# Block transposes on VectorE in place of TensorE transposes in the last phase of a Fourier-operator kernel

## The chip, the cores and the metric

One NeuronCore of a Trainium2 chip runs the whole kernel as one program. The metric is the device time of one execution in microseconds; the times shown are medians of runs. TensorE is called PE (its weight loads PEld), VectorE DVE, ScalarE ACT, GpSimd POOL, and SyncE SP. Accumulators lie in PSUM, here as four tensors of two banks each (pA, pT, pD, pS); everything else lies in SBUF.

## What is computed

An image of 64 x 64 pixels and 3 channels goes through a spectral network (64 images, width 32, four layers), and the result, read as 4096 tokens of 64 numbers, goes through four token layers (attention, experts, a recurrent layer, experts). The change touches the end of the first part and the image load:

```
h = layer_norm(x @ fc0_w + fc0_b)
for i in range(4):
    h = spectral_conv(h, w1[i], w2[i]) + conv1x1(h, conv_w[i]) + conv_b[i]
    h = layer_norm(h)
    if i < 3: h = gelu(h)
h = gelu(h @ fc1_w + fc1_b)     # 32 -> 128
h = gelu(h @ fc2_w + fc2_b)     # 128 -> 64
h = (h @ fc3_w + fc3_b)[..., 0] # 64 -> 1
```

All values are float32.

## The kernel before, in words

**Groups and bodies.** The 64 images are worked on in 16 groups of 4. A group in the last spectral layer consists of steps with short names: `i1.0` and `i1.1` (inverse transform in y), `acc.0` to `acc.3` (inverse transform in x and the 1x1 convolution, accumulated in pA), a copy of each `acc` to SBUF by ACT (the tile `raw`), `sq` (squares, ACT), `red` (sums, DVE), `rs` (reciprocal root, seven small DVE operations, L207 to L213), `scale` (normalising `raw`, DVE, L1638), `turn.0` to `turn.3`, then the output layers `fc1.0` to `fc1.7`, `fc2.0` to `fc2.15`, `fc3.0`, `fc3.1`, `fin.0` and `fin.1`.

**What turn and fin do.** `raw[n]` holds rows (pixels) on partitions. `turn.n` (PE, L1317) makes eight 128 x 128 transposes of it into pA, and DVE copies pA to the tile `h_new` (L1646). `fin.h` (PE, L1405) makes four 128 x 128 transposes of `G3`, the copied result of `fc3.h`, into a half of pT, and two ACT instructions add the bias and put the wanted columns into the token tile (L1513).

**The output layers.** `fc1.u` (L1374) reads 512 columns of `h_new` in four strips of 32 partitions: strips 0 and 1 write the two banks of pD, strips 2 and 3 the two banks of pS. ACT takes pD and pS in one GELU each (L1496, `fc1.2u` and `fc1.2u+1`) into two buffers `G1`. `fc2.m` (L1385) reads one of these and writes a half of pT; ACT's GELU (L1499) takes it to one of eight slots of `G2`. `fc3.h` (L1395) reads eight slots, ACT copies the result to `G3` (L1502).

**Order.** Each engine has its own instruction queue, and the order of the steps in each queue is written out by hand in the table `ORDER`, for each phase. A trailing minus marks a step of the group before. The order `into_last` ends the layer before and starts group 0 of the last phase. Then a body runs the output layers of one group beside the image work of the next: 15 bodies in the order `last` (one by itself, fourteen in a loop), and after them a body with the late steps of the last group alone. Before the first body come the mixing matmuls of the layer (L1217) and POOL's store of their result, after which POOL clears the tiles of the token parameters. PE's order in a body, before:

```
fc2.0- fc1.1- fc2.1- i1.1 fc2.2- fc1.2- fc2.3- turn.2- fc2.4- fc1.3- fc2.5- i1.0 fc2.6- fc1.4-
fc2.7- turn.3- fc3.0- fc1.5- fc2.8- fc2.9- acc.0 fc2.10- fc1.6- fc2.11- acc.1 fc2.12- fc1.7- acc.2
fc2.13- fc2.14- acc.3 fc2.15- fin.0- turn.0 fc3.1- fc1.0 fin.1- turn.1
```

**Waits.** PSUM tensors are handed out as rings: pA (ring "a", one slot) to `i1`, `acc` and `turn`, the halves of pT (ring "r", two slots) to `fc2`, `fc3` and `fin`. A PE step waits until the one that had its slot before is taken. `fc1.u` waits for the copy of `turn.(u//2)` and until both GELUs of the `fc1` before have read pD and pS; `fc2.m` waits for the GELU of `fc1` into its buffer; `fc3.h` waits until ACT has taken its eight `fc2`; `acc.n` waits for DVE's transpose of `i1` (L1617).

Of the kernel before, what the change touches and what calls it, by code (L numbers as in the profile page):

```python
# [51 lines left out]
def constants():  # L52
# [77 lines left out]
    "h_new":         (4, 0, 4, 4),  # L130
    "x_in":          (16, 0, 0, 0),
    "y_in":          (0, 0, 128, 128),
# [25 lines left out]
    "into_last": {  # L158
        "PE": ("i1.1 turn.2- back.1- i1.0 acc.0 turn.3- back.2- acc.1 back.3- acc.2 f1.1- f1.0- acc.3 f2.0- f2.1- "
               "mix.0 turn.0 fc1.0 turn.1"),  # L160
        "ACT": ("gelu.2- back.1- acc.0 sq.0 gelu.3- back.2- acc.1 sq.1 back.3- acc.2 sq.2 acc.3 sq.3 pack.0- pack.1- "
                "mix.0 fc1.0 fc1.1"),
        "DVE": ("red.3- i1.1 rs.3- scale.3- i1.0 red.0 rs.0 scale.0 red.1 rs.1 f1.1- scale.1 red.2 f1.0- f2.0- f2.1- "
                "mix.0 turn.0"),
    },
    "last": {
# [9 lines left out]
    },  # L176
# [4 lines left out]
    "mid": dict(i1="d", back="s", f1="d", f2="d"),  # L181
    "last": dict(i1="a", acc="a", turn="a", fc2="r", fc3="r", fin="r"),
}
# [32 lines left out]
def build(nc, ins, out_ap, B):  # L216
# [18 lines left out]
    with ctx:  # L235
# [77 lines left out]
        def param(rows, cols):  # L313
# [47 lines left out]
                 "w_centred", "mix_a_full", "mix_a_free", "mix_b_full", "mix_b_free", "y_bias", "conv_cleared", "conv_loaded", "conv_turned", "conv_chain", "cst_loaded", "ln_loaded",  # L361
                 "fc0_loaded", "fc0_chain", "mlp_cleared", "mlp_loaded", "normed", "eps_set"]
        names += ["td_full", "td_free", "ts_full", "ts_free", "par_cleared", "par_loaded", "tok_ready", "v_chain", "shifted",
# [171 lines left out]
        def token_act(act):  # L535
# [8 lines left out]

            act.wait_ge(s["r_free"], 20 * NG + 2)
            act.sem_inc(s["tok_ready"], 1)
# [423 lines left out]
        def _(sp):  # L970
            def load_x(g):
                src = ins["x"].rearrange("(g t b) y x c -> g (b y) t (x c)", t=2, b=2)
                sp.dma_start(x_in, src[g]).then_inc(s["x_loaded"], 16)

# [35 lines left out]
            def mlp_params():  # L1010
                sp.wait_ge(s["mlp_cleared"], 1)
                for j in range(4):
                    sp.dma_start(fc1_w[32 * j:32 * j + 32, :],
                                 ins["L0_tok_fc1_w"]).then_inc(s["mlp_loaded"], 16)
                sp.dma_start(fc1_b, ins["L0_tok_fc1_b"].rearrange("(p o) -> p o", o=1)).then_inc(s["mlp_loaded"], 16)
                sp.dma_start(fc2_w, ins["L0_tok_fc2_w"]).then_inc(s["mlp_loaded"], 16)
                for j in range(2):
                    q = slice(64 * j, 64 * j + 64)
                    sp.dma_start(fc2_b[q], ins["L0_tok_fc2_b"].rearrange("(p o) -> p o", o=1)).then_inc(s["mlp_loaded"], 16)
                    for k in range(2):  # L1020
                        sp.dma_start(fc3_pad[q, k, 2 * k + j:2 * k + j + 1], ins["L0_tok_fc3_w"]).then_inc(s["mlp_loaded"], 16)
                sp.dma_start(fc3_b, ins["L0_tok_fc3_b"].partition_broadcast(P)).then_inc(s["mlp_loaded"], 16)
# [161 lines left out]
        def _(pe):  # L1184
# [43 lines left out]
            def steps(p):  # L1228
# [12 lines left out]
                def xt(n, g):  # L1241

                    pe.wait_ge(s["x_loaded"], at("x_in", ph, L, g, 16))
                    bank = bank_of("xt", n, g)
# [62 lines left out]
                def turn(n, g):  # L1307

                    pe.wait_ge(s["normed"], at("normed", ph, L, g, n + 1))
                    if ph == "last":  # L1310
                        bank = bank_of("turn", n, g)
                    else:
                        bank = pT
                        if n >= 1 or not first_group(g):
                            pe.wait_ge(s["h_new_ok"], at("h_new", ph, L, g, n))
                    for j in range(8):
                        mm = pe.transpose(bank[:, 128 * j:128 * j + 128], raw[n][:, 128 * j:128 * j + 128], ident)  # L1317
                    if ph == "last":
                        send(mm, "turn", n, g)
                    else:  # L1320
                        mm.then_inc(s["turned"], 1)

# [39 lines left out]
                def fc1(u, g):  # L1362
# [25 lines left out]
                def fc3(h, g):  # L1388
# [10 lines left out]
                def fin(h, g):

                    p.taken(pe, ("fc3", h), g=g)
                    alone(pe)
                    bank = bank_of("fin", h, g)
                    for j in range(4):
                        mm = pe.transpose(bank[:, 128 * j:128 * j + 128], G3[:, 128 * j:128 * j + 128], ident)  # L1405
                    send(mm, "fin", h, g)
# [9 lines left out]
        def _(act):  # L1416
# [18 lines left out]
            def steps(p):  # L1435
# [64 lines left out]

                def fc3(h, g):
                    act.copy(G3, take("fc3", h, g)).then_inc(s["r_free"], 1)  # L1502

                def fin(h, g):

                    bank = take("fin", h, g)
                    if first_group(g):
                        act.wait_ge(s["y_stored"], 64 * 2 * LAYERS)
                    alone(act)
                    out = tok[:, bass.ds(g * 128, 128)].rearrange("p (t a q n) -> p t a q n", t=2, a=4, q=4)  # L1510
                    src = bank.rearrange("p (q a t r) -> p t a q r", q=4, a=2, t=2)
                    for t in range(2):
                        ins_ = act.activation(out[:, t, 2 * h:2 * h + 2], src[:, t, :, :, 0:4], ACT.Identity, bias=fc3_b)  # L1513
                    ins_.then_inc(s["r_free"], 1)

# [7 lines left out]
        def _(dve):  # L1523
# [84 lines left out]
            def steps(p):  # L1608
# [85 lines left out]
```

## Time and profile before

| what | value |
| --- | --- |
| median of three runs | 3279.34 us (3277.0 to 3285.81) |
| span of the profiled execution | 3279.2 us |
| PE busy | 2937.9 us (90%) |
| PE weight loads busy | 1867.7 us (57%) |
| DVE busy | 2145.9 us (65%) |
| ACT busy | 1950.3 us (59%) |
| POOL busy | 61.9 us (2%) |

The profiled execution's own time is its span, 3279.2 us from the first to the last instruction; outside it no separate number is shown. Busy times overlap between engines. "Idle before" names the time that an engine stood still ahead of an instruction and what ended it. A timeline row gives the start, the length, the instruction with its output and input tiles, and how many neighbours are merged into it; PE records of neighbouring instructions overlap, so a pitch is best taken from starts. The last phase runs from about 1905 to 2659 us.

### The profile page before, as it was taken

Reading aid. Unit: us, or ns where it says so; the run is one execution under the profiler, and the core shown is the slowest. Engines: PE = TensorE matmul, PEld = TensorE weight load, DVE = VectorE, ACT = ScalarE, POOL = GpSimd, SP = SyncE. Lnnn points to the kernel's source line nnn. Section 1 sums busy time; section 2 is a strip of 40 time slices with the busy share of each in tenths; the row PEclk is TensorE's granted clock in tenths of the full one; section 3 lists DMA queues with packets and bytes.
Section 4 is the critical chain, followed back from the end, with each engine's and each line's share of the span. In section 5 each row is a group of like instructions: output and inputs, shape, how many; then the busy total and the mean of one; then the engine's idle time right before and its main releaser. Section 6 shows DMA issues by size and latency. Waiting matters only on the chain.

```text
span 3279.2 us, 82177 instructions
## 1 busy us (share of the span) xinstructions
PE 2937.9 (90%) x32240; PEld 1867.7 (57%) x32240; DVE 2145.9 (65%) x3954; ACT 1950.3 (59%) x2271; POOL 61.9 (2%) x81
## 2 busy tenths in 40 slices
PE   7888889999889999889999889999999987964994
PEld 3545466666666666666666544444444447952893
DVE  6888668888668888668888644454445434255457
ACT  6777656666556666556666457777777753422451
POOL 0000000000000000000000010000000001000000
PEclk9999999999999999999999999999999998986897
DMA  3422346544447544546544423111111000000000
GB/s 96 130 97 99 100 152 209 193 165 164 152 130 218 183 164 163 155 154 209 179 165 164 151 67 86 46 55 58 46 46 55 29 1 1 1 1 0 1 1 13
DMA packets 98093, 335.91 MB, mean 102 GB/s; under 512 B 29928, under 2 KB 61960, under 8 KB 62088
## 3 DMA queue, kind: packets, MB, share of 16 engines
q1 hardware_dynamic: 75400, 161.50, 16.4%
q10 hardware_dynamic: 18432, 134.23, 10.0%
q0 software_dynamic: 4096, 37.75, 5.3%
q8 instruction: 131, 2.15, 0.3%
q14 instruction: 34, 0.28, 0.0%
HBM read 179.29 MB, written 154.14 MB: 102 GB/s over the span
## 4 chain that ended last, share of the span: by engine, by line
PE 79%; DVE 11%; issue 5%; ACT 5%; DVEq 0%; SPq 0%; DMA 0%; ACTq 0%
PE pA L1291 15%; PE pA L1299 8%; PE pT L1385 8%; PE pT L1317 5%; PE pS L1328 5%; PE pD L1342 4%; PE pD L1374 4%; PE pD L1356 4%; PE pD L467 3%; PE pA L467 3%; PE pD L1263 3%; PE pA L1281 3%; PE pS L459 2%; PE pT L459 2%; DVE arena L1657 2%
## 5 line engine op out<-in xcount | busy, mean ns | idle before, releaser
L1624 DVE TENSOR_REDUCE small<-arena 128x32 f32<-128x1056 f32 x320 | 397.0, 1241 | 316.0 <-ACT arena L1461 311.3
L1291 PEld LDWEIGHTS pA<-conv_bd,h_in 128*128 128x128 f32 x4096 | 479.0, 192 | 109.4 <-issue 92.7
L1291 PE MATMUL pA<-conv_bd,h_in 128*128 128x128 f32 x4096 | 517.4, 280 | 8.6 <-DVE arena L1617 2.9
L1451 ACT COPY w_sb<-pA 128x1024 f32<-128x1024 f32 x256 | 259.8, 1015 | 393.0 <-PE pA L1299 343.3
L1638 DVE SCALAR_TENSOR_TENSOR w_sb<-w_sb,small 128x1024 f32<-128x1024 f32 x320 | 386.8, 1213 | 5.5
L1472 ACT ACTIVATE h_new<-pT,bet,gam 128x1024 f32<-128x1024 f32 x256 | 307.5, 1201 | 100.2 <-PE pT L1317 92.1
L1461 ACT ACTIVATE arena<-w_sb 128x1024 f32<-128x1024 f32 x320 | 339.3, 1060 | 13.4
L1317 PEld LDWEIGHTS pT<-cst,w_sb 128*128 128x128 f32 x2048 | 225.2, 143 | 144.5 <-issue 123.9
L1317 PE MATMUL pT<-cst,w_sb 128*128 128x128 f32 x2048 | 283.0, 282 | 23.2 <-DVE w_sb L1638 23.2
L1476 ACT COPY h_rows<-pS 128x1024 f32<-128x1024 f32 x256 | 257.1, 1004 | 64.9 <-PE pS L1328 64.6
L1328 PEld LDWEIGHTS pS<-cst,h_new 128*128 128x128 f32 x2048 | 228.5, 143 | 113.0 <-issue 71.6
L1328 PE MATMUL pS<-cst,h_new 128*128 128x128 f32 x2048 | 275.4, 278 | 9.4 <-ACT h_new L1472 9.4
L1299 PE MATMUL pA<-arena,cst 64*64 64x512 f32 x2048 | 278.8, 615 | 0.0
L1385 PE MATMUL pT<-w_sb,arena 128*64 128x512 f32 x1024 | 270.3, 616 | 2.7 <-ACT w_sb L1499 1.5
L1356 PE MATMUL pD<-arena,cst 64*32 64x384 f32 (+1 forms) x4096 | 206.8, 491 | 10.2 <-DVE arena L1657 9.8
L1499 ACT ACTIVATE w_sb<-pT,arena 128x512 f32<-128x512 f32 x256 | 173.1, 685 | 16.5 <-PE pT L1385 15.4
L1496 ACT ACTIVATE w_sb<-pD,arena 128x1024 f32<-128x1024 f32 x128 | 142.5, 1113 | 63.1 <-PE pD L1374 39.3
L1657 DVE STREAM_TRANSPOSE arena<-pD 128x768 f32<-128x768 f32 x128 | 125.5, 981 | 78.4 <-PE pD L1356 62.5
L1342 PE MATMUL pD<-h_rows,cst 64*32 64x512 f32 x2048 | 139.7, 600 | 36.2 <-DVE arena L1651 21.2
L1651 DVE STREAM_TRANSPOSE arena<-pD 128x1024 f32<-128x1024 f32 x128 | 159.3, 1245 | 4.9 <-PE pD L1342 1.1
L1617 DVE STREAM_TRANSPOSE arena<-pD 128x1024 f32<-128x1024 f32 x96 | 119.8, 1248 | 47.9 <-PE pD L1263 47.3
L1374 PE MATMUL pD<-h_new,arena 32*128 32x512 f32 x512 | 145.5, 644 | 3.6 <-issue 1.7
(299 smaller groups left out, 3903.0 us busy)
## 6 DMA issues: line engine op xcount, KB each, us to landing
h_scratch<-h_new ACTq DMA_DIRECT2D x128, 1024.0 KB, 4.5
h_in<-h_scratch SPq DMA_DIRECT2D x128, 1024.0 KB, 5.1
y_scratch<-w_sb POOLq DMA_DIRECT2D x32, 576.0 KB, 8.4
y_in<-y_scratch SPq DMA_DIRECT2D x512, 36.0 KB
w_sb<-in_L_tok_w1r_dram POOLq DMA_DIRECT2D x8, 576.0 KB, 7.0
w_sb<-in_L_tok_w1i_dram POOLq DMA_DIRECT2D x8, 576.0 KB, 6.7
w_sb<-in_L_tok_w2r_dram POOLq DMA_DIRECT2D x8, 576.0 KB, 8.3
w_sb<-in_L_tok_w2i_dram POOLq DMA_DIRECT2D x8, 576.0 KB, 7.7
```

What stands on the lines that cost most here:

```text
L1291: pe.matmul(pA[:, c:c + 128], h_in[:, 1024 * n + c:1024 * n + c + 128], conv_bd[:], start=(j == 0), stop=False, skip_group_check=True)
L1299: mm = pe.matmul(pA[64 * b:64 * b + 64, 512 * t:512 * t + 512].rearrange("p (x o) -> p o x", o=C), const["idft_y"][rows, 64 * b:64 * b + 6 ...
L1317: mm = pe.transpose(bank[:, 128 * j:128 * j + 128], raw[n][:, 128 * j:128 * j + 128], ident)
L1328: mm = pe.transpose(bank[:, 128 * j:128 * j + 128], h_new[:, 1024 * n + 128 * j:1024 * n + 128 * j + 128], ident)
L1342: mm = pe.matmul(out[q:q + 32, b], const["dft_y"][rows, NQ * b:NQ * b + NQ], src[rows, t, 32 * xh:32 * xh + 32, 16 * ch:16 * ch + 16], sta ...
L1356: mm = pe.matmul(out.rearrange("p (q h c) -> p h c q", h=2, c=16), const["dft_x"][rows, 128 * part + 32 * j:128 * part + 32 * j + 32], TA[ ...
L1374: mm = pe.matmul(out, fc1_w[rows, :], h_new[rows, 512 * u:512 * u + 512], start=True, stop=True)
L1385: mm = pe.matmul(bank[64 * j:64 * j + 64, :], fc2_w, G1[m % 2][:, 512 * j:512 * j + 512], start=True, stop=True)
L1461: act.activation(sq[n % 2][:, :, 0:C], raw[n].rearrange("p (x o) -> p x o", o=C), ACT.Square, scale=float(C) ** -0.5).then_inc(s["squared" ...
L1472: act.activation(h_new[:, 1024 * n:1024 * n + 1024], pT[:], ACT.Gelu if ph == "mid" else ACT.Identity, bias=bet[:, col], scale=gam[:, col] ...
L1624: dve.reduce_sum(var[n], sq[n % 2], axis=AX).then_inc(s["summed"], 1)
L1638: dve.scalar_tensor_tensor(out=z, in0=z, scalar=ROOT_SCALE, in1=r.broadcast_to([P, 32, C]), op0=ALU.mult, op1=ALU.mult).then_inc(s["normed ...
```

## The change

In the last phase `turn` becomes one DVE block transpose (blocks of 32 x 32 on 128 partitions) from `raw` to `h_new`, and the PE transposes and DVE copies go. `fin` loses its PE part: DVE block-transposes `G3` into a new tile `G3_t`, and one ACT instruction takes the wanted columns. Because block transposes leave each strip of 32 partitions with other pixels than before, the image load is laid out anew (two DMAs of 64 partitions per group), `fc1`'s matmuls write their strips to other banks, and `fc3`'s take their slots of `G2` in another order. The rings lose `turn` and `fin`, the orders lose the PE steps, DVE gets `fc3.0-` and `fc3.1-`, and new waits stand in ACT's `acc`, `fc3` and `fin` and in DVE's `turn` and `fc3`.

```diff
-    "x_in":          (16, 0, 0, 0),
+    "x_in":          (32, 0, 0, 0),
...
     "into_last": {
-        "PE": ("... f2.1- mix.0 turn.0 fc1.0 turn.1"),
+        "PE": ("... f2.1- mix.0 fc1.0"),
...
     "last": {
-        "PE": the order quoted above
+        "PE": ("fc2.0- fc1.1- fc2.1- i1.1 fc2.2- fc1.2- fc2.3- fc2.4- fc1.3- fc2.5- i1.0 fc2.6- fc1.4- fc2.7- fc3.0- fc1.5- fc2.8- fc2.9- acc.0 fc2.10- fc1.6- fc2.11- acc.1 fc2.12- fc1.7- acc.2 fc2.13- fc2.14- acc.3 fc2.15- fc3.1- fc1.0"),
-        "DVE": ("rs.2- scale.2- turn.1- i1.1 red.3- turn.2- rs.3- scale.3- i1.0 turn.3- red.0 red.1 rs.0 rs.1 red.2 "
-                "scale.0 scale.1 turn.0"),
+        "DVE": ("rs.2- scale.2- turn.1- i1.1 red.3- turn.2- rs.3- scale.3- i1.0 turn.3- fc3.0- red.0 red.1 rs.0 rs.1 red.2 scale.0 turn.0 scale.1 fc3.1-"),
...
-    "last": dict(i1="a", acc="a", turn="a", fc2="r", fc3="r", fin="r"),
+    "last": dict(i1="a", acc="a", fc2="r", fc3="r"),
...
+        G3_t = w_sb[:, 3584:4096]
...
-                src = ins["x"].rearrange("(g t b) y x c -> g (b y) t (x c)", t=2, b=2)
-                sp.dma_start(x_in, src[g]).then_inc(s["x_loaded"], 16)
+                src = ins["x"].rearrange("(g b t) y x c -> g b y t (x c)", t=2, b=2)
+                for b in range(2):
+                    sp.dma_start(x_in[64 * b:64 * b + 64], src[g][b]).then_inc(s["x_loaded"], 16)
...
                 def fc1(u, g):
-                    for j in range(4):
-                        rows = slice(32 * j, 32 * j + 32)
-                        out = (pD, pS)[j // 2][:, 512 * (j % 2):512 * (j % 2) + 512]
...
+                    for k in range(2):
+                        for b in range(2):
+                            rows = slice(64 * b + 32 * k, 64 * b + 32 * k + 32)
+                            mm = pe.matmul((pD, pS)[k][:, 512 * b:512 * b + 512], fc1_w[rows, :], h_new[rows, 512 * u:512 * u + 512],
+                                           start=True, stop=True)
+                        mm.then_inc(s["s_full" if k else "d_full"], 1)
...
                 def acc(n, g):          # ACT
                     if ph == "last":
                         p.in_turn(act, "acc", n, g)
+                        if not first_group(g):
+                            act.wait_ge(s["h_new_ok"], at("h_new", ph, L, g, n - 3))
+                            alone(act)
...
                 def fc3(h, g):          # ACT
+                    if h or not first_group(g):
+                        act.wait_ge(s["g3_turned"], 2 * g + h)
+                        alone(act)
                     act.copy(G3, take("fc3", h, g)).then_inc(s["r_free"], 1)

                 def fin(h, g):          # ACT
-                    bank = take("fin", h, g)
+                    act.wait_ge(s["g3_turned"], 2 * g + h + 1)
...
+                    out = tok[:, bass.ds(g * 128, 128)].rearrange("p (b h n x) -> p b h n x", b=2, h=2, n=2)
+                    src = G3_t.rearrange("p (x r) -> p r x", r=32)[:, 0:4, :].rearrange("p (b n) x -> p b n x", b=2)
+                    act.activation(out[:, :, h], src, ACT.Identity, bias=fc3_b).then_inc(s["fin_done"], 1)
...
                 def turn(n, g):         # DVE
-                    p.in_turn(dve, "turn", n, g)
-                    dve.tensor_copy(h_new[:, 1024 * n:1024 * n + 1024], take("turn", n, g)).then_inc(s["a_free"], 1)
-                    p.taken(dve, ("turn", n), g=g)
-                    dve.sem_inc(s["h_new_ok"], 1)
+                    if not first_group(g):
+                        dve.wait_ge(s["s_full"], p.quad("s", 2 * n + 1, g - 1))
+                        alone(dve)
+                    dve.wait_ge(s["normed"], at("normed", ph, L, g, n + 1))
+                    dve.transpose(h_new[:, 1024 * n:1024 * n + 1024], raw[n]).then_inc(s["h_new_ok"], 1)
+
+                def fc3(h, g):
+
+                    p.taken(dve, ("fc3", h), g=g)
+                    if h or not first_group(g):
+                        alone(dve)
+                        dve.wait_ge(s["fin_done"], 2 * g + h)
+                    dve.transpose(G3_t, G3).then_inc(s["g3_turned"], 1)
```

## Rows read from the trace of the kernel before

**Rows 1.** Windows by engine: start:end, length, PE, PEld, DVE, ACT, POOL busy (count), clock, DMA.

```profile
1964.20:2623.60 659.40, 657.42 (x5043) 283.84 (x5042) 309.21 (x589) 510.03 (x645) 0.00 (x0) 1.00 0.18 52
...
2623.60:2659.40 35.80, 31.34 (x178) 9.21 (x178) 7.76 (x14) 28.04 (x39) 0.00 (x0) 1.00 0.00 1
```

**Rows 2.** Lines of the fourteen steady bodies: count, busy us, mean ns, idle before.

```profile
L1317 PE MATMUL pA<-cst,w_sb 128*128 128x128 f32 x449 | 59.9, 276 | 0.0
...
L1405 PE MATMUL pT<-cst,w_sb 128*128 128x128 f32 x112 | 18.4, 286 | 0.0
...
L1617 DVE STREAM_TRANSPOSE arena<-pA 128x1024 f32<-128x1024 f32 x28 | 34.9, 1246 | 37.5 <-PE pA L1263 37.5
```

**Rows 3.** Timeline of one steady body, PE, ACT and DVE: start, us, instruction.

```profile
2098.41 1.08 PE L1385 MATMUL pT<-w_sb,arena 128*64 128x512 f32 x4
...
2100.88 1.92 PE L1395 MATMUL pT<-w_sb,arena 128*32 128x512 f32 x16
...
2102.94 0.70 PE L1374 MATMUL pD<-h_new,arena 32*128 32x512 f32 x2
...
2102.95 0.70 PE L1374 MATMUL pS<-h_new,arena 32*128 32x512 f32 x2
...
2105.54 1.08 PE L1385 MATMUL pT<-w_sb,arena 128*64 128x512 f32 x4
...
2110.48 0.70 PE L1374 MATMUL pD<-h_new,arena 32*128 32x512 f32 x2
...
2113.59 1.08 PE L1385 MATMUL pT<-w_sb,arena 128*64 128x512 f32 x4
...
2119.59 1.08 PE L1385 MATMUL pT<-w_sb,arena 128*64 128x512 f32 x4
...
2121.69 1.92 PE L1395 MATMUL pT<-w_sb,arena 128*32 128x512 f32 x16
...
2102.87 0.59 ACT L1502 COPY w_sb<-pT 128x512 f32<-128x512 f32 x1 [1.34 <-PE pT L1395]
...
2103.11 0.18 DVE L207 TENSOR_SCALAR small<-small 128x32 int32<-128x32 int32 x1 [0.82 <-DVE h_new L1646]
...
2105.82 1.22 DVE L1646 COPY h_new<-pA 128x1024 f32<-128x1024 f32 x1
```

**Rows 4.** Timeline of PE in the late-only last body.

```profile
2624.59 0.70 PE L1374 MATMUL pD<-h_new,arena 32*128 32x512 f32 x2
...
2627.03 1.08 PE L1385 MATMUL pT<-w_sb,arena 128*64 128x512 f32 x4 [0.28 <-ACT w_sb L1496]
...
2628.11 0.70 PE L1374 MATMUL pD<-h_new,arena 32*128 32x512 f32 x2
...
2653.32 1.08 PE L1385 MATMUL pT<-w_sb,arena 128*64 128x512 f32 x4 [0.50 <-ACT w_sb L1499]
...
2655.28 1.92 PE L1395 MATMUL pT<-w_sb,arena 128*32 128x512 f32 x16 [0.29 <-ACT w_sb L1499]
```

**Rows 5.** Timeline of the entry into the last phase: PE, DVE, POOL.

```profile
1905.52 1.83 PE L1317 MATMUL pA<-cst,w_sb 128*128 128x128 f32 x8 [1.13 <-ACT w_sb L1432]
...
1907.50 1.23 DVE L1646 COPY h_new<-pA 128x1024 f32<-128x1024 f32 x1 [5.53 <-PE pA L1317]
...
1907.92 7.08 POOL L1173 MEMSET spec<- 128x8358 f32 x1
...
1909.03 1.22 PE L1374 MATMUL pD<-h_new,arena 32*128 32x512 f32 x2 [1.67 <-issue]
...
1909.08 5.97 DVE L207 TENSOR_SCALAR small<-small 128x32 int32<-128x32 int32 x1 [0.36 <-DVE h_new L1646]
...
1918.90 1.28 PE L1263 MATMUL pA<-y_in,cst 48*32 48x208 f32 x32 [3.00 <-issue]
...
1923.41 1.08 PE L1385 MATMUL pT<-w_sb,arena 128*64 128x512 f32 x4
```

**Rows 6.** Timeline of PE at the program's start.

```profile
14.07 3.75 PE L1281 MATMUL pA<-arena 128*128 128x512 f32 x4 [7.79 <-DVE arena L1539]
```

More of the change, by code:

```diff
@@ L158 @@
     "into_last": {
[L159 to L164, printed above, removed]
[3 rows of a table added]
     },
     "last": {
[9 rows of a table removed]
[3 rows of a table added]
     },
@@ L361, in build @@
                  "w_centred", "mix_a_full", "mix_a_free", "mix_b_full", "mix_b_free", "y_bias", "conv_cleared", "conv_loaded", "conv_turned", "conv_chain", "cst_loaded", "ln_loaded",
-                 "fc0_loaded", "fc0_chain", "mlp_cleared", "mlp_loaded", "normed", "eps_set"]
+                 "fc0_loaded", "fc0_chain", "mlp_cleared", "mlp_loaded", "g3_turned", "fin_done", "normed", "eps_set"]
         names += ["td_full", "td_free", "ts_full", "ts_free", "par_cleared", "par_loaded", "tok_ready", "v_chain", "shifted",
@@ L542, in take @@
                 return TS[(n[0] - 1) % 4]
-            act.wait_ge(s["r_free"], 20 * NG + 2)
+            act.wait_ge(s["fin_done"], 2 * NG)
             act.sem_inc(s["tok_ready"], 1)
@@ L1020, in mlp_params @@
                     for k in range(2):
-                        sp.dma_start(fc3_pad[q, k, 2 * k + j:2 * k + j + 1], ins["L0_tok_fc3_w"]).then_inc(s["mlp_loaded"], 16)
+                        sp.dma_start(fc3_pad[q, k, 2 * j + k:2 * j + k + 1], ins["L0_tok_fc3_w"]).then_inc(s["mlp_loaded"], 16)
                 sp.dma_start(fc3_b, ins["L0_tok_fc3_b"].partition_broadcast(P)).then_inc(s["mlp_loaded"], 16)
@@ L1241, in xt @@
                 def xt(n, g):
-                    pe.wait_ge(s["x_loaded"], at("x_in", ph, L, g, 16))
+                    pe.wait_ge(s["x_loaded"], at("x_in", ph, L, g, 32))
                     bank = bank_of("xt", n, g)
@@ L1309, in turn @@
                     pe.wait_ge(s["normed"], at("normed", ph, L, g, n + 1))
[L1310 to L1315, printed above, removed]
-                    for j in range(8):
[L1317 to L1321, printed above, removed]
+                    if n >= 1 or not first_group(g):
+                        pe.wait_ge(s["h_new_ok"], at("h_new", ph, L, g, n))
+                    for j in range(8):
+                        mm = pe.transpose(pT[:, 128 * j:128 * j + 128], raw[n][:, 128 * j:128 * j + 128], ident)
+                    mm.then_inc(s["turned"], 1)
                 def back(n, g):
@@ L1370, in fc1 @@
                     alone(pe)
-                    for j in range(4):
-                        rows = slice(32 * j, 32 * j + 32)
-                        out = (pD, pS)[j // 2][:, 512 * (j % 2):512 * (j % 2) + 512]
-                        mm = pe.matmul(out, fc1_w[rows, :], h_new[rows, 512 * u:512 * u + 512], start=True, stop=True)
-                        if j % 2:
-                            mm.then_inc(s["d_full" if j == 1 else "s_full"], 1)
+                    for k in range(2):
[4 more added lines that the diff above has]
+                        mm.then_inc(s["s_full" if k else "d_full"], 1)
                 def fc2(m, g):
@@ L1392, in fc3 @@
                     bank = bank_of("fc3", h, g)
-                    for k in range(2):
+                    for part in range(2):
                         for u in range(4):
-                            mm = pe.matmul(bank[32 * u:32 * u + 32, :], fc3_pad[:, k, :], G2[:, 2 * u + k, :],
-                                           start=(k == 0), stop=(k == 1), skip_group_check=True)
+                            mm = pe.matmul(bank[32 * u:32 * u + 32, :], fc3_pad[:, part, :], G2[:, 4 * part + u, :],
+                                           start=(part == 0), stop=(part == 1), skip_group_check=True)
                     send(mm, "fc3", h, g)
[L1399 to L1406, printed above, removed]
                 return dict(xt=xt, i1=i1, acc=acc, turn=turn, back=back, f1=f1, f2=f2,
-                            fc1=fc1, fc2=fc2, fc3=fc3, fin=fin)
+                            fc1=fc1, fc2=fc2, fc3=fc3)
             phases(pe, "PE", mix, steps)
@@ L1501, in fc3 @@
                 def fc3(h, g):
+                    if h or not first_group(g):
+                        act.wait_ge(s["g3_turned"], 2 * g + h)
+                        alone(act)
                     act.copy(G3, take("fc3", h, g)).then_inc(s["r_free"], 1)
                 def fin(h, g):
-                    bank = take("fin", h, g)
+                    act.wait_ge(s["g3_turned"], 2 * g + h + 1)
+                    alone(act)
                     if first_group(g):
                         act.wait_ge(s["y_stored"], 64 * 2 * LAYERS)
[L1509 to L1514, printed above, removed]
+                    out = tok[:, bass.ds(g * 128, 128)].rearrange("p (b h n x) -> p b h n x", b=2, h=2, n=2)
+                    src = G3_t.rearrange("p (x r) -> p r x", r=32)[:, 0:4, :].rearrange("p (b n) x -> p b n x", b=2)
+                    act.activation(out[:, :, h], src, ACT.Identity, bias=fc3_b).then_inc(s["fin_done"], 1)
                 return dict(xt=xt, acc=acc, sq=square, gelu=gelu, back=back, pack=pack, fc1=fc1, fc2=fc2, fc3=fc3, fin=fin)
@@ L1658, in f2 @@
                                   bank.rearrange("p (t n) -> p t n", t=2)[:, :, 0:384]).then_inc(s["d_free"], 1)
-                return dict(cen=cen, i1=i1, red=red, rs=rs, scale=scale, turn=turn, f1=f1, f2=f2)
+                return dict(cen=cen, i1=i1, red=red, rs=rs, scale=scale, turn=turn, fc3=fc3, f1=f1, f2=f2)
             phases(dve, "DVE", mix, steps, conv_centre, centring)
```

11 rows, old and new, of the table ORDER are left out of this document.

## Prediction

> **What bounds the kernel now.** I read the stretches first, then the waits inside them, then the order of one body. Fourteen steady bodies of the last phase fill 659.4 us, 47.1 us each; TensorE (PE) is busy for 657.42 us of that at clock 1.00, VectorE (DVE) for 309.21 and ScalarE (ACT) for 510.03 [rows 1]. So PE sets this phase, and PE work taken out can shorten it, but only as far as nothing else ends just behind it. "PE busy" does not show that; it is read from starts. The busy PE hides ACT: a GELU has to come back from ACT before PE may go on, and an instruction that stands in the gap looks like work, although the gap would be there without it. The late-only last body, which has no image work, shows it: PE idles 0.28 us in front of one fc2 and 0.29 us in front of fc3 [rows 4].
>
> **What is removed from PE, and what comes back.** Per body, 32 transposes of images and 8 of tokens go. Their busy time over 14 bodies is 59.9 and 18.4 us, so 4.28 and 1.31 us per body, 5.6 together [rows 2] (records of neighbours overlap, so the starts give some 0.5 less). If all of it came back, 15 bodies would give some 80 us. I take each place apart by starts in rows 3, against what the same chain needs where nothing stands between.
>
> - turn.2 between fc2.3 and fc2.4. fc2.4 needs the GELU of fc1.2's first bank. From the start of an fc1 to the fc2 that waits for its GELU the bare chain takes 2627.03 - 2624.59 = 2.44 us [rows 4]. From fc1.2 to fc2.4 it is now 2113.59 - 2110.48 = 3.11 [rows 3]. Gain 0.67, not the 1.0 of turn.2.
> - turn.3 between fc2.7 and fc3.0. fc3 waits for the GELU of the last fc2: bare, 2655.28 - 2653.32 = 1.96 [rows 4]; now 2121.69 - 2119.59 = 2.10 [rows 3]. Gain 0.14.
> - fin.0 and turn.0 between fc2.15 and fc3.1: now 2100.88 - 2098.41 = 2.47 [rows 3], bare 1.96. Gain 0.51.
> - fc3.1 to fc1.0 is 2.06; fc3's own pitch is at most its 1.92, with the overlap some 1.85 [rows 3]. fc1.0 waited for DVE's copy of turn.0, which now is early. Gain 0.14 to 0.21.
> - fin.1 and turn.1 between fc1.0 and fc2.0: now 2105.54 - 2102.94 = 2.60 [rows 3], bare 2.44. Gain 0.16, where 1.5 us of PE work go.
>
> Sum 1.62 to 1.69. Against it: an fc2 begun after a wait holds PE for 1.08 (2627.03 to 2628.11 [rows 4]), one that was queued for 1.01 or less; four places at 0.07 each make 0.28 at most. Per body 1.35 to 1.7, I take 1.5; fourteen bodies 21 us (19 to 24). What is late next at every place is ACT's GELU.
>
> **What DVE takes on.** Four copies from PSUM of 1.22 us [rows 3] become four block transposes from SBUF, and two transposes of 512 columns come in. No row has a 1024-column transpose from SBUF: bounds are a copy's 1.22 and double the 1.25 of the transpose from PSUM [rows 2], 2.5; I take 1.25, the same operation and size, and 0.7 for half. DVE has half of its time free [rows 1], so only one place counts. The transpose of G3 (fc3.1) waits for ACT's copy, and rs.2, scale.2 and turn.1 are queued behind it, and PE's fc1.2 behind turn.1. From fc3.1's start: ACT's copy at +1.99, 0.59 long, DVE at about +2.75, G3 done at +3.45, rs.2 and scale.2 take 2105.82 - 2103.11 = 2.71, turn.1 1.25: +7.4, with a semaphore +7.55 [rows 3]. PE reaches fc1.2 at 1.85 + 2.44 + (2110.48 - 2105.54) = +9.2. Slack 1.7 us, which the doubled price (1.95 more) would just use up: nothing, or 0.3 per body. ACT's fin waits for G3's transpose too, but two GELUs stand before it. ACT's copy of an image result gets a wait for the transpose of the group before, which ran a body earlier: nothing.
>
> **Banks of fc1 and fc3.** The same matmuls in another order. The four of fc1 begin 0.01 us apart in pD and pS [rows 3], together. Each keeps a row strip and a bank of its own, so I take nothing; the other bound is pairs one after the other, near 1 us for each of 128, and below zero there is no cause for a gain.
>
> **Entry into the phase.** After the mixing matmuls, PE runs turn.0 at 1905.52, once ACT has emptied its bank; DVE had been idle 5.53 us when it began the copy at 1907.50, so since 1901.97; fc1.0 begins at 1909.03 [rows 5]. Now DVE can transpose at 1902 and be done by 1903.4, and fc1.0 begins at 1905.5, when the bank is free: 3.5 us. Then rs.2's first operation took 5.97 us instead of 0.18, while a POOL memset from 1907.92 ran 7.08 us; that made turn.1 late, which holds pA, and PE sat 3.00 us in front of i1.1 at 1918.90 [rows 5]. With turn.0 done at 1903.4, rs.2 is through near 1905, turn.1 near 1907.5, before the memset, and i1.1 no longer waits for pA: 3.0 us. The PE records at 1909.03 are 1.22 long against 0.70 [rows 3, 5], so PE runs slowly there; the new first ops meet that too, and turn.1 as warm-up is gone. That may cost 1 to 2 us, the second slow spell behind the 3 us gap gives about as much back. Entry 6.5 us; between 3 (the stall stays) and 7.5.
>
> **The rest.** The first body's interior lacks some of the waits above: 1.1. The last body loses turn.2, 0.6; in its tail a PE turn is swapped for a DVE turn of like length. The image load becomes two DMA issues on SP; at the start PE's first accumulation waits for DVE's setup chain (7.79 us idle before 14.07 [rows 6]), behind which half a microsecond of SP is hidden, and later loads run a group ahead. If that cover were gone: one issue per group, well under 1 us each. Zero.
>
> **Sum:** 6.5 + 1.1 + 21 + 0.6 = 29.2 us from the profiled span of 3279.2, which lies 0.14 below the median of the runs, 3279.34. Forecast 3250.
>
> **PE's clock.** With 1.3 to 1.4 us waits at two places and 0.9 at two more, PE would be some 92% busy. In the last body PE is busy 31.34 of 35.8 us, 88%, with the same kind of gaps, and the granted clock is 1.00 [rows 1]. The Trainium skill ("TensorE: Matmul & The Clock Gate", "A second HAM failure mode: psum-queue depth-cycling") tells of a kernel whose short idles between matmul groups made the clock swing between its levels. By that rule the change would lose, the rival below; the rows speak against it.
>
> **Rivals.**
> 1. All of PE's removed time comes back: 3279 - 80 - 7 = 3192. For it: PE is the bound everywhere. Against it: the bare chains of rows 4. 3%.
> 2. The new queue on DVE: if the transposes from SBUF cost three times 1.25, turn.1 comes 3.9 us later, 2.2 past its slack, more than the body's 1.5. Entry gain only, some 3272 to 3282. Nothing but the missing row speaks for it. 6%.
> 3. Slower: PE's short waits bring the clock down. A PE instruction at the low level takes nearly twice as long. With a fifth of the 700 us at 1.2 GHz (mean 0.90) a tenth of the work is lost, some 76 us: 3250 + 76 = 3326. It decides from a mean clock of about 0.96, where it eats the 29 us. 5%. By the Trainium skill's rule on short idles this would be the outcome; rows 1 are against it.
> 4. The entry keeps its stall and bodies give 1.2: 3279 - 3 - 17 - 1 = 3258, inside the range.
>
> **Numbers.** The likeliest case with its variants holds 86%: 7.5 + 24 + 1.7 = 33 off gives 3246, 3258 the other end; the bounds of the transposes and the spread of runs (3277.0 to 3285.8) widen this to 3238 to 3264. A measurement here can tell about 0.3%, 10 us, from no change. Faster 0.86 (with rival 1), same 0.08, slower 0.06.
>
> **What would show it.** Right: bodies of about 45.6 us; PE idle before fc2.4, fc3.0, fc3.1 and fc2.0, each put down to an ACT GELU; no 3 us gap before i1.1; clock 1.00. Wrong: fc1.2 waiting for DVE; a granted clock under 0.97 in the steady bodies; an fc1 pitch over 1.1 us; bodies under 44 us.

## The result, and the profile after

| | before | after |
| --- | --- | --- |
| median | 3281.58 us (3277.0 to 3285.81) | 3260.07 us (3258.54 to 3262.73) |
| profiled span | 3279.2 us | 3256.7 us |

The ratio of the times is 0.9931, with a 95% interval of 0.9918 to 0.9944. The changed kernel is faster, by 21.5 us between the medians and 22.5 us between the profiled spans, where 29 were forecast. The measured 3260 lies inside the range and 10 us above the forecast figure; 2.2 of these 10 come from the median of the kernel before, which is 3281.58 here and was 3279.34 in the forecast. The medians and ratios below leave out four executions with a lower mean granted clock (3379.61 to 3673.02 us, one of the kernel before and one each in runs 5, 6 and 8), and of run 8 only the last phase is read, which lies ahead of the fall of its clock.

Cut at the same instructions, the two profiled executions give:

| stretch | before | after | gain | forecast |
| --- | --- | --- | --- | --- |
| start to last mixing matmul | 1903.28 | 1906.14 | -2.86 | 0 |
| last mixing matmul to fc2.3 | 20.13 | 13.85 | 6.28 | 6.5 |
| fc2.3 to the first steady body | 40.79 | 39.76 | 1.03 | 1.1 |
| fourteen steady bodies | 659.40 | 643.44 | 15.96 | 21 |
| last body, fc2.0 to fc3.1 | 31.68 | 31.01 | 0.67 | 0.6 |
| fc3.1 to the end | 623.92 | 622.50 | 1.42 | 0 |
| sum | 3279.2 | 3256.7 | 22.5 | 29.2 |

The windows of the kernel after, over its fourteen steady bodies and its last body (start:end, length, then busy time and count of PE, PEld, DVE, ACT, POOL, the granted clock, DMA), answer to [rows 1]:

```profile
1959.75:2603.19 643.44, 589.22 (x4481) 223.58 (x4481) 325.85 (x616) 508.84 (x617) 0.00 (x0) 1.00 0.18 54
2603.19:2638.31 35.12, 28.25 (x153) 6.76 (x154) 10.39 (x19) 27.74 (x36) 0.00 (x0) 1.00 0.00 1
```

PE is now busy 589.22 of 643.44 us, 91.6%, and the clock stays at 1.00. Some 68 us of PE's busy time went, 16 us of the time. The rest is PE's idle time, which the grouped lines of the same stretch put down to ACT's two GELUs (count | busy, mean ns | idle before and its releaser):

```profile
L1371 PE MATMUL pT<-w_sb,arena 128*64 128x512 f32 x897 | 236.1, 614 | 27.2 <-ACT w_sb L1476 27.2
...
L1381 PE MATMUL pT<-w_sb,arena 128*32 128x512 f32 x448 | 53.9, 598 | 28.4 <-ACT w_sb L1479 28.4
...
L1630 DVE STREAM_TRANSPOSE h_new<-w_sb 128x1024 f32<-128x1024 f32 x56 | 68.8, 1229 | 0.5
...
L1638 DVE STREAM_TRANSPOSE w_sb<-w_sb 128x512 f32<-128x512 f32 x28 | 19.9, 712 | 85.6 <-ACT w_sb L1485 85.6
```

The first two rows hold 55.6 us of idle, which accounts for all that PE has (643.44 - 589.22 = 54.2 by the windows). fc2 waits for the GELU of fc1 (L1476), fc3 for the GELU of fc2 (L1479). The last two rows give the prices that no row of before had: 1.23 us for a transpose of 1024 columns from SBUF, 0.71 for one of 512.

Timeline of one steady body of the kernel after, PE: fc2.0, fc1.2 and the fc2.4 that waits for it, fc2.7 and fc3.0, fc2.15 and fc3.1, fc1.0, the next fc2.0 and the fc1.1 behind it; it answers to [rows 3].

```profile
2097.69 1.08 PE L1371 MATMUL pT<-w_sb,arena 128*64 128x512 f32 x4 [1.43 <-ACT w_sb L1476]
...
2102.63 0.70 PE L1360 MATMUL pD<-h_new,arena 32*128 32x512 f32 x2
...
2105.20 1.08 PE L1371 MATMUL pT<-w_sb,arena 128*64 128x512 f32 x4 [0.42 <-ACT w_sb L1476]
...
2111.21 1.08 PE L1371 MATMUL pT<-w_sb,arena 128*64 128x512 f32 x4
2113.31 1.92 PE L1381 MATMUL pT<-w_sb,arena 128*32 128x512 f32 x16 [1.01 <-ACT w_sb L1479]
...
2137.14 1.08 PE L1371 MATMUL pT<-w_sb,arena 128*64 128x512 f32 x4
2139.24 1.92 PE L1381 MATMUL pT<-w_sb,arena 128*32 128x512 f32 x16 [1.01 <-ACT w_sb L1479]
2141.09 0.70 PE L1360 MATMUL pD<-h_new,arena 32*128 32x512 f32 x2
...
2143.66 1.08 PE L1371 MATMUL pT<-w_sb,arena 128*64 128x512 f32 x4 [1.43 <-ACT w_sb L1476]
2144.67 0.70 PE L1360 MATMUL pD<-h_new,arena 32*128 32x512 f32 x2
```

A body takes 2143.66 - 2097.69 = 45.97 us, in place of 47.1. PE stands at exactly the four places that were named. But the chains are longer than the bare ones that the sum used: fc1 to its waiting fc2 takes 2.57 twice (2105.20 - 2102.63, 2143.66 - 2141.09) where [rows 4] gave 2.44, and fc2 to fc3 takes 2.10 twice where they gave 1.96.

The entry into the phase in the kernel after answers to [rows 5]: turn.0 and rs.2's first operation on DVE, the last mixing matmul, fc1.0, POOL's first memset, fc2.0, i1.1, a second memset, fc1.2, a reduction on DVE, fc2.3, fc2.4, and a third memset with rs.3's first operation under it.

```profile
1905.02 1.23 DVE L1630 STREAM_TRANSPOSE h_new<-w_sb 128x1024 f32<-128x1024 f32 x1
...
1906.14 1.11 PE L1210 MATMUL pS<-w_sb,spec 64*32 64x64 f32 x53 [1.49 <-issue]
1906.18 0.14 DVE L198 TENSOR_SCALAR small<-small 128x32 int32<-128x32 int32 x1
...
1908.70 0.70 PE L1360 MATMUL pD<-h_new,arena 32*128 32x512 f32 x2 [1.45 <-ACT w_sb L1409]
...
1910.78 7.08 POOL L1166 MEMSET spec<- 128x8358 f32 x1
...
1911.12 1.97 PE L1371 MATMUL pT<-w_sb,arena 128*64 128x512 f32 x4 [1.28 <-ACT w_sb L1476]
...
1916.95 1.03 PE L1256 MATMUL pA<-y_in,cst 48*32 48x208 f32 x32
...
1917.92 3.51 POOL L1169 MEMSET h_rows<- 64x4096 f32 x1
...
1918.92 0.70 PE L1360 MATMUL pD<-h_new,arena 32*128 32x512 f32 x2
...
1919.36 1.21 DVE L1605 TENSOR_REDUCE small<-arena 128x32 f32<-128x1056 f32 x1
...
1919.99 1.08 PE L1371 MATMUL pT<-w_sb,arena 128*64 128x512 f32 x4
...
1921.35 1.08 PE L1371 MATMUL pT<-w_sb,arena 128*64 128x512 f32 x4 [0.28 <-ACT w_sb L1476]
...
1921.49 3.50 POOL L1171 MEMSET h_rows<- 1x4096 f32 x1
1921.64 3.39 DVE L198 TENSOR_SCALAR small<-small 128x32 int32<-128x32 int32 x1
```

turn.0 runs before the last mixing matmuls begin on PE and is through just behind their start, the first operation of rs.2 takes 0.14 us because it is through before the memset, and nothing idles before i1.1. The operation that a memset holds is now rs.3's (3.39 us), where nobody waits for it. PE has a slow spell of its own here: after two idles of 1.45 and 1.28 us the granted clock is 0.50, the lower of its two levels, from 1911.12 to 1915.00, and fc2.0 takes 1.97 us in place of 1.08. One more thing is to be seen here: this first body is not in the loop, and its chain from fc1.2 to fc2.4 is 1921.35 - 1918.92 = 2.43, as in [rows 4].

### The profile page after: what moved, and what is told of

Its sections match the earlier page's. It is cut to its first block, busy times and chain, and to the rows that moved or that the text cites. A ratio compares the mean times of both kernels' runs of the same rounds, so it can differ in the third digit from the quotient of the medians.

```text
span 3256.7 us, 80827 instructions
## 1 busy us (share of the span) xinstructions
PE 2861.2 (88%) x31600; PEld 1798.1 (55%) x31600; DVE 2161.4 (66%) x3986; ACT 1948.1 (60%) x2239; POOL 61.9 (2%) x81
## 4 chain that ended last, share of the span: by engine, by line
PE 76%; DVE 11%; ACT 7%; issue 5%; DVEq 0%; SPq 0%; DMA 0%; ACTq 0%
PE pA L1284 15%; PE pA L1292 8%; PE pT L1371 7%; PE pT L1306 5%; PE pS L1314 5%; PE pD L1328 4%; PE pD L1360 4%; PE pD L1342 4%; PE pD L459 3%; PE pA L459 3%; PE pA L1274 3%; PE pD L1256 3%; PE pS L451 2%; PE pT L451 2%; DVE arena L1647 2%
## 5 line engine op out<-in xcount | busy, mean ns | idle before, releaser
L1479 ACT ACTIVATE w_sb<-pT,arena 128x512 f32<-128x512 f32 x256 | 171.3, 685 | 8.0 <-PE pT L1371 6.3
L1476 ACT ACTIVATE w_sb<-pD,arena 128x1024 f32<-128x1024 f32 x128 | 142.4, 1112 | 55.4 <-PE pD L1360 31.6
L1371 PEld LDWEIGHTS pT<-w_sb,arena 128*64 128x64 f32 x1024 | 54.0, 135 | 213.8 <-issue 112.6
```

What stands on the lines that cost most here:

```text
L1371: mm = pe.matmul(bank[64 * j:64 * j + 64, :], fc2_w, G1[m % 2][:, 512 * j:512 * j + 512], start=True, stop=True)
```

## The experiments

**Theory before the runs:** PE's removed work comes back only where it exceeded ACT's round trip, and inside the loop each such stall costs about 0.13 us more than in the bodies that are written out. **Rivals:** the 0.13 belongs to the body (more neighbours, other work on ACT) and not to the loop; or the new transposes on DVE hold something.

**1. The changed kernel with its loop written out.**

```diff
-            with eng.Fori(2, NG) as b:
+            for b in range(2, NG):
                 at_body(b)
```

> The changed kernel with the fourteen steady bodies of the last phase written out instead of looped, so that every wait there is against a constant; nothing else. In the loop each place where PE waits for ACT takes 0.13 to 0.15 us more than the same place in the first and last bodies, which are not looped (2.57 against 2.43 us from an fc1 to the fc2 behind its GELU, 2.10 against 1.95 from an fc2 to fc3). Theory A, the loop's waits (values that PE's sequencer works out at the wait) make that difference: bodies fall from 45.97 to 45.4 us, the time by 7 to 8 us, to about 3252. Rival B, the difference is ACT's, from the image work beside it: bodies stay at 45.97, the time at 3260. Rival C, longer code has to be fetched and costs more than it gives: bodies above 46, time above 3262.

Measured: 3252.84 us (3252.14 to 3258.17), ratio to before 0.9915 (0.9898 to 0.9931). The timeline of PE in one body, from fc3.1 to the next fc3.1:

```profile
2089.64 1.92 PE L1381 MATMUL pT<-w_sb,arena 128*32 128x512 f32 x16 [0.88 <-ACT w_sb L1479]
...
2093.93 1.08 PE L1371 MATMUL pT<-w_sb,arena 128*64 128x512 f32 x4 [1.29 <-ACT w_sb L1476]
...
2101.30 1.08 PE L1371 MATMUL pT<-w_sb,arena 128*64 128x512 f32 x4 [0.28 <-ACT w_sb L1476]
2102.39 0.70 PE L1360 MATMUL pD<-h_new,arena 32*128 32x512 f32 x2
...
2109.35 1.92 PE L1381 MATMUL pT<-w_sb,arena 128*32 128x512 f32 x16 [0.88 <-ACT w_sb L1479]
...
2135.14 1.92 PE L1381 MATMUL pT<-w_sb,arena 128*32 128x512 f32 x16 [0.88 <-ACT w_sb L1479]
```

A body takes 45.50 us. Each of the four idles is 0.13 or 0.14 shorter than in the loop, and the chains are the bare ones. So the missing 0.13 per place belongs to the loop. Over fourteen bodies that is 6.6 us; the two ratios, 0.9931 and 0.9915, differ by 5 us, a little less than the 7 to 8 that were expected. What in the loop costs this was not taken apart and stays open.

**2. The kernel before with its loop written out** (the same edit).

> The kernel before with the same fourteen bodies written out. Theory A: PE had work in its queue at four of the five places, so the waits' values were ready in time; bodies of 47.1 us fall by 0 to 0.15, the time by 0 to 2 us. Rival: the loop costs PE time at every instruction, wait or not; then bodies fall as much as in the changed kernel, the time by 7 us or more.

Measured: 3277.33 us, ratio 0.9977 (0.9965 to 0.9990); bodies of 46.78 us (fc3.1 at 2105.74 and 2152.52). The loop costs the kernel before 0.32 a body, less than the 0.47 of the changed one, but more than the 0 to 0.15 that were expected. The time alone could not have told: the ratio stands for 7.5 us with an interval of 3.3 to 11.5, and fourteen bodies give 4.5. From fc3.1 to fc2.0 it takes 4.39 in place of 4.66, and turn.3's pitch falls from 1.09 to 1.02. The profile shows no idle at these places, so what was shortened there is argued and not shown: the steps that start earlier are fc1.0, which needs DVE's copy of turn.0, and fc2.0 and fc3.0, which need a GELU. If these are short stalls behind PE's own work, the expectation missed that the kernel before already had them.

**3 and 4. Work put into the idle places.** Eight transposes of the identity into pA (results not used) in front of fc3.0, and in another kernel in front of fc2.4. pA is free there.

```diff
-  fc2.7- fc3.0-
+  fc2.7- fill.1 fc3.0-
...
-  fc2.3- fc2.4-
+  fc2.3- fill.0 fc2.4-
...
+                def fill(n, g):
+                    bank_of(("i1", "acc")[n], 0, g)
+                    alone(pe)
+                    for j in range(8):
+                        pe.transpose(pA[:, 128 * j:128 * j + 128], ident, ident)
```

> The changed kernel with eight 128 x 128 transposes of the constant identity into pA put back where turn.3 stood, between fc2.7 and fc3.0; nobody reads them. PE idles 1.01 us there. Theory: the gap belongs to ACT's GELU, so PE's work in it costs nothing: bodies stay at 45.97 us (up to 46.1), the time within 2 us of the changed kernel. Rival: PE's work costs what it lasts: bodies of 47.0, 15 us more.

> The same eight transposes put back where turn.2 stood, between fc2.3 and fc2.4, where PE idles only 0.42 us. Theory: they cost what they last over the gap, 3.11 - 2.57 = 0.54 us per body: bodies of 46.5, some 8 us over the changed kernel. Rival, PE's work counts in full: 1.0 per body, 15 us. Rival, it is hidden altogether: no change.

Measured, with one execution each: in front of fc3.0 nothing changes (span 3256.7 us, bodies 45.97). In front of fc2.4 the span is 3265.0 and a body 46.52. PE of the second, the added transposes and fc2.4 behind them:

```profile
2144.40 0.70 PE L1360 MATMUL pD<-h_new,arena 32*128 32x512 f32 x2
...
2146.48 1.09 PE L1390 MATMUL pA<-cst 128*128 128x128 f32 x8
2147.50 1.08 PE L1371 MATMUL pT<-w_sb,arena 128*64 128x512 f32 x4
```

fc1.2 to fc2.4 is 3.10, as before the change (3.11), against 2.57: turn.2 was worth 0.53 a body, and turn.3, an equal instruction group, nothing. That is the prediction's way of counting, with 2.57 in place of 2.44.

**5. The kernel before with POOL's memsets later.**

```diff
             pool.wait_ge(s["mix_b_full"], 6 * LAYERS)
+            pool.wait_ge(s["normed"], at("normed", "last", LAYERS - 1, 0, 4))
             pool.memset(spec[:, 0:at_col[0]], 0.0).then_inc(s["par_cleared"], 1)
```

> Kernel before; only POOL's clearing of the token parameters (three memsets, the first 7.08 us long) waits until DVE has normalised the last rows of group 0, some 15 us later. Theory: the first operation of rs.2 was held by the memset, and everything up to the 3.00 us gap before i1.1 followed from it. Then that operation takes about 0.2 us in place of 5.97, the gap before i1.1 is gone, and from the last mixing matmul to fc2.3 it takes 16.5 to 17.5 us in place of 20.13: the whole kernel 2.5 to 3.5 us shorter, all of it in that stretch. Rival: the operation was slow for another reason (first use after a phase change), or i1.1 waited for something else: the stretch stays at 20 us.

Measured: 3278.68 us (3273.74 to 3283.68), ratio 0.9983 (0.9973 to 0.9993). Timeline of the entry:

```profile
1904.19 1.14 PE L1218 MATMUL pS<-w_sb,spec 64*32 64x64 f32 x53 [1.28 <-issue]
...
1909.81 1.22 PE L1375 MATMUL pD<-h_new,arena 32*128 32x512 f32 x2 [1.67 <-issue]
...
1909.85 0.18 DVE L207 TENSOR_SCALAR small<-small 128x32 int32<-128x32 int32 x1 [0.34 <-DVE h_new L1647]
...
1916.77 0.91 PE L1264 MATMUL pA<-y_in,cst 48*32 48x208 f32 x32
...
1919.69 1.08 PE L1386 MATMUL pT<-w_sb,arena 128*64 128x512 f32 x4
...
1926.47 7.07 POOL L1174 MEMSET spec<- 128x8358 f32 x1 [17.61 <-DVE w_sb L1639]
```

The operation takes 0.18 us, the gap before i1.1 is gone, and the stretch is 1919.69 - 1904.19 = 15.50 us in place of 20.13. The memset alone was worth 4.63 us in this profile, more than the 3.0 put on it and than the 2.5 to 3.5 expected of the run: with the gap the second slow spell went too (i1.1 takes 0.91 us in place of 1.28), which the prediction had set off against other losses. So the change's 6.28 us at the entry are only 1.65 more than one could have had by moving a memset. This holds for these profiles only. The stretch moves with where the clock is low: it is 20.13 and 20.88 us in the two profiles of the kernel before with early memsets, and 11.03 to 14.68 in the nine of the changed kernel and its variants.

**6 and 7. Closing the two largest idles.** In the changed kernel fc1.0 goes ahead of fc3.1, so that each covers the other's GELU; ACT's and DVE's orders follow, with fin.0, turn.1 and red.2 at other places. Once with the loop, once written out.

```diff
-        "PE": ("... acc.3 fc2.15- fc3.1- fc1.0"),
+        "PE": ("... acc.3 fc2.15- fc1.0 fc3.1-"),
-        "ACT": ("... fc1.14- acc.2 ... acc.3 fc2.15- sq.3 fin.0- fc3.1- fc1.0 fc1.1 fin.1-"),
+        "ACT": ("... fc1.14- fin.0- acc.2 ... acc.3 fc2.15- fc1.0 fc1.1 fc3.1- sq.3 fin.1-"),
-        "DVE": ("rs.2- scale.2- turn.1- ... rs.0 rs.1 red.2 scale.0 turn.0 scale.1 fc3.1-"),
+        "DVE": ("rs.2- scale.2- ... rs.0 rs.1 scale.0 turn.0 scale.1 turn.1 red.2 fc3.1-"),
```

> Changed kernel with the end of a body re-ordered: on PE fc1.0 of the next group runs ahead of fc3.1, ACT takes the two GELUs of fc1 ahead of the copy of fc3.1, and DVE runs turn.1 at the end of the body it belongs to. Theory (PE waits at this place only for ACT's round trip, 1.01 us before fc3.1 and 1.43 before fc2.0): fc1.0 and fc3.1 cover each other's GELU, both gaps close, a body takes 43.5 to 43.8 us in place of 45.97 and the kernel about 3226 (3222 to 3230). Rival (something else ends just behind, ACT's queue or the ring of pT): the wait moves to fc2.1, fc1.2 or the next fc2 and a body stays at 45 or more, 3246 or more.

> The kernel of the run with fc1.0 ahead of fc3.1, its fourteen bodies also written out in place of the loop. Theory (a loop adds about 0.13 us to each place where PE stalls on a semaphore): with two stalls left per body (before fc2.4 and before fc3.0) instead of four, a body loses 0.2 to 0.3 us against the looped one, 3 to 4 us in all. Rival (the loop costs the same per body wherever PE stalls): 0.47 us per body as without the re-ordering, 6 to 7 us.

Measured: 3226.83 us (3225.41 to 3234.12) with the loop, ratio to before 0.9823 (0.9804 to 0.9843); 3221.14 written out, 0.9804 (0.9788 to 0.9821). Both beat the changed kernel. With the loop, PE's timeline from fc2.2 to the next fc2.2, and the ACT instruction that the new wait comes from:

```profile
2140.32 1.08 PE L1371 MATMUL pT<-w_sb,arena 128*64 128x512 f32 x4 [0.39 <-ACT w_sb L1476]
...
2143.89 1.08 PE L1371 MATMUL pT<-w_sb,arena 128*64 128x512 f32 x4 [0.42 <-ACT w_sb L1476]
...
2152.00 1.92 PE L1381 MATMUL pT<-w_sb,arena 128*32 128x512 f32 x16 [1.01 <-ACT w_sb L1479]
...
2177.93 1.92 PE L1381 MATMUL pT<-w_sb,arena 128*32 128x512 f32 x16
...
2184.17 1.08 PE L1371 MATMUL pT<-w_sb,arena 128*64 128x512 f32 x4 [0.39 <-ACT w_sb L1476]
```

```profile
2181.85 0.40 ACT L1495 ACTIVATE w_sb<-w_sb,arena 128x64 f32 x1 [0.29 <-DVE w_sb L1638]
```

A body takes 43.86 us, 2.11 less and just outside the 43.5 to 43.8 that were expected; the time is inside its range. The 1.01 before fc3.1 and the 1.43 before fc2.0 are gone, 2.44 as expected, and a new 0.39 stands before fc2.2: ACT's queue now has copy, sq.3 and fin.1 between the GELUs, and fin.1 waits 0.29 for DVE's transpose of G3. Moving fin.1 was not tried. Written out, a body takes 43.20 us (fc2.4 to fc2.4), 0.66 less, which neither the theory nor its rival gave:

```profile
2135.49 1.08 PE L1371 MATMUL pT<-w_sb,arena 128*64 128x512 f32 x4 [0.28 <-ACT w_sb L1476]
...
2143.53 1.92 PE L1381 MATMUL pT<-w_sb,arena 128*32 128x512 f32 x16 [0.88 <-ACT w_sb L1479]
...
2178.69 1.08 PE L1371 MATMUL pT<-w_sb,arena 128*64 128x512 f32 x4 [0.28 <-ACT w_sb L1476]
```

0.14 and 0.13 come at the two old places, as the theory says; the other 0.4 or so is the 0.39 before fc2.2, which is not there. In the written-out run DVE's transpose of G3 begins 0.14 us after ACT's copy has ended (0.32 in the loop), and fin.1 starts at 2173.12 with no idle before it. So the queues of DVE and ACT run shorter too, and the theory had counted only PE's stalls.

**8 to 10. DVE's slack.** turn.1 transposed three times, and twice, into the same place.

```diff
                 def turn(n, g):         # DVE
...
+                    if n == 1:
+                        dve.wait_ge(s["normed"], at("normed", ph, L, g, n + 1))
+                        alone(dve)
+                        dve.sem_clear(s["root_chain"])
+                        for k in range(2):
+                            dve.transpose(h_new[:, 1024 * n:1024 * n + 1024], raw[n]).then_inc(s["root_chain"], 1)
+                            dve.wait_ge(s["root_chain"], k + 1)
```

> Changed kernel; DVE makes the block transpose of turn.1 three times in a row into the same place, some 2.6 us more in its queue ahead of PE's fc1.2. Theory (the slack of this place is 1.7 us, 2146.80 to 2148.60 in the trace less the semaphore): fc1.2 waits for DVE, and a body grows by 0.8 to 1.0 us, to about 46.9, the kernel by some 12 to 15 us. Rival A (slack was larger, the fc2.4 behind waits for ACT anyway): bodies 46.0 to 46.2. Rival B (DVE's queue already sets the body): bodies 48.5.

> Changed kernel; DVE makes the block transpose of turn.1 twice, 1.3 us more in its queue ahead of PE's fc1.2. Theory (slack 1.7 us at this place): fully hidden, bodies 45.97 as in the changed kernel. Rival (the slack is only what the run with three transposes left uncovered, and the semaphores take more): bodies grow by 0.2 us or more.

> The kernel with three transposes of turn.1 once more, now for its time: in the first look its bodies were 46.99 us, 1.02 more than in the changed kernel, and the token phase ran at a low clock that the edit has nothing to do with. Theory: bodies 46.99 again, and the whole 14 to 16 us above the changed kernel, 3272 to 3277. Rival (the longer DVE queue brings the clock down later on): the token phase slow again, over 3300.

Measured: twice, span 3254.3 us in one execution and bodies of 45.97, as without the edit. Three times, bodies of 46.99 in run 8 and 47.02 in run 10; run 10 takes 3274.48 us, ratio 0.9973 (0.9959 to 0.9987), which is 0.0042, 14 us, above the changed kernel's ratio. The rival's time, over 3300, did not come (3265.88 to 3286.05 in ten executions). DVE and PE of run 8:

```profile
2148.39 2.52 DVE L1635 STREAM_TRANSPOSE h_new<-w_sb 128x1024 f32<-128x1024 f32 x2
2150.94 1.25 DVE L1637 STREAM_TRANSPOSE h_new<-w_sb 128x1024 f32<-128x1024 f32 x1
```

```profile
2150.53 1.08 PE L1371 MATMUL pT<-w_sb,arena 128*64 128x512 f32 x4
2152.58 0.70 PE L1360 MATMUL pD<-h_new,arena 32*128 32x512 f32 x2 [0.97 <-DVE h_new L1637]
```

The three end at 2152.19 and take 3.80 us, 2.56 more than one; fc1.2 starts at 2152.58 and not at 2150.53 + 1.01 = 2151.54, 1.04 late. So the slack was 2.56 - 1.04 = 1.5 us, and the body grew by what goes beyond it (1.02). One transpose more, 1.3 us, stays inside the slack, as the run with two showed.

## Why the prediction was right, and where its sum was off

**What bounds the phase: right.** PE was busy everywhere, yet only a quarter of what was taken from it came back. The runs that fill the idle places (0.00 and 0.53 for equal work) show for the places of turn.3 and turn.2 that the rest covered ACT's GELU, and the run with fc1.0 ahead of fc3.1 shows it for the two larger idles, which work put between closes. Rival 1, all 80 us, falls.

**The bodies: the mis-sized term.** By the five places of the working:

| place | forecast | measured |
| --- | --- | --- |
| fc1.2 to fc2.4 (turn.2) | 0.67 | 3.11 - 2.57 = 0.54 |
| fc2.7 to fc3.0 (turn.3) | 0.14 | 2.10 - 2.10 = 0.00 |
| fc2.15 to fc3.1 (fin.0, turn.0) | 0.51 | 2.47 - 2.10 = 0.37 |
| fc3.1 to fc1.0 | 0.14 to 0.21 | 2.06 - 1.85 = 0.21 |
| fc1.0 to fc2.0 (fin.1, turn.1) | 0.16 | 2.60 - 2.57 = 0.03 |

The step that was off is "the bare chain takes 2.44" and "bare, 1.96" [rows 4]. These were read in the last body, which stands outside the loop; in the loop they are 2.57 and 2.10, at four places, 0.54 a body. The 0.28 set against the sum, for an fc2 begun after a wait, did not come in the loop: from such an fc2 to the next instruction it is 1.01 (2143.66 to 2144.67). Together 1.13 in place of 1.5, and over fourteen bodies 16 in place of 21. The run with the loop written out brings the bare chains back, and at fc2.4 also the 1.09 after a wait (2101.30 to 2102.39): 45.50 us a body, 1.6 less than the looped kernel before, where the places had summed to 1.62 to 1.69 and the forecast took 1.5.

**The entry: right in size, 6.28 for 6.5.** Cut at the start of fc1.0, its two parts came as said. From the last mixing matmul to fc1.0 it takes 2.56 in place of 5.75 us, 3.19 for the forecast 3.5; from there to fc2.3 it takes 11.29 in place of 14.38, 3.09 for 3.0. The cause named for the second, a memset that holds one DVE operation, is shown by the run with the memsets late, where that part falls to 9.88 and the one ahead of fc1.0 stays at 5.62. Against that run the change gains 3.06 ahead of fc1.0 and loses 1.41 behind it, where its own slow spell at fc2.0 stands; 1.65 is left. That the slow spells would cancel was a guess, and that they nearly did is luck: in run 10, whose clock is 1.00 from the last mixing matmul to fc2.3, the whole stretch takes 11.03 us in place of 13.85. Rival 4, 3258 us, lies nearer to the measured time than the forecast does; it had the bodies nearly right with 1.2 and the entry wrong, for no stall is left before i1.1.

**DVE: right.** The transposes cost 1.23 and 0.71 us where 1.25 and 0.7 were taken; the slack is 1.5 for 1.7. Rival 2 is out by its condition, transposes of three times 1.25. Its mechanism is real: with turn.1 alone at that length fc1.2 waits for DVE, and 1.02 of the body's 1.13 is lost again.

**Image load, banks: nothing, as said.** PE's first accumulation starts where it did in [rows 6], with half a microsecond less idle before it:

```profile
14.03 3.75 PE L1274 MATMUL pA<-arena 128*128 128x512 f32 x4 [7.21 <-DVE arena L1520]
```

From fc1 to the fc2 queued behind it is 1.07 in both kernels.

**The clock: right.** It is 1.00 through the fourteen steady bodies, with four waits of 0.4 to 1.4 us in each. The rule of the Trainium skill ("TensorE: Matmul & The Clock Gate", "A second HAM failure mode: psum-queue depth-cycling"), by which short idles make the clock swing, does not show there: from 1960 to 2560 us the clock is 1.00 in all twelve profiles of this study. Rival 3 falls with it.

**What was counted as zero and wasn't.** The last phase began 2.86 us later than before, and what follows it took 1.42 less. Neither can be put down to the change. Over the profiles whose edits leave the phases ahead alone, the last mixing matmul begins at 1903.28, 1904.19 and 1908.15 in the kernel before and its two variants, and between 1899.32 and 1909.59 in the changed kernel and eight profiles of its variants. From fc3.1 to the end it takes 621.2 to 629.5 us over the same profiles without run 8. A single pair of profiles can't tell 3 us there. The phase alone, from the last mixing matmul to fc3.1, gained 23.9 us.

## What to carry to other kernels

Before counting removed work as time, take each place where it stood and compare it with the shortest chain of the other engines across it; what lies under that chain is cover and returns nothing. Read that chain in the same kind of code as the place itself, looped or written out, because the stall has its own price there. Where the chain is what is left, put independent work into it (here fc1.0 ahead of fc3.1, some 30 us) rather than take work off the engine that waits.

## What the runs showed of the hardware

- A stall on a semaphore costs more inside this kernel's loop over the steady bodies than in the same code written out: 0.13 to 0.14 us at each of four places on PE (1.43 against 1.29, 1.01 against 0.88 twice, 0.42 against 0.28). Instructions that are queued without a stall keep their pitch (fc1 1.07, fc2 1.01).
- A POOL memset held one kind of DVE operation until its end: L207 from 1909.08 to 1915.05 under a memset that ended at 1915.00 [rows 5], L198 from 1921.64 to 1925.03 under one that ended at 1924.99. A block transpose of 1.25 us (from 1918.18) and a reduction of 1.21 (from 1919.36) ran in the changed kernel under the memset from 1917.92 to 1921.43 and kept their usual length. The Trainium skill ("SBUF — State Buffer", "Who interferes with whom") says that VectorE and GpSimd share a port pair which one of them holds for a whole instruction, that tensor_scalar is among the operations that can ask for it, and that a reduction is not; these rows agree.
- A DVE block transpose from SBUF takes what one from PSUM does: 1.23 against 1.25 us for 128 x 1024 values [rows 2].
